# A graph network's ODE solver with its two weight products per step folded into one: six-layer local pass, mid stages without a product

## The reference, cut to what matters

```
def gcn(x, W, b):                    # edges src -> dst, deg = edges in + 1, dinv = rsqrt(deg)
    h = x @ W
    agg = segment_sum(h[src] * (dinv[src] * dinv[dst]), dst)
    return agg + dinv * dinv * h + b
x = l2norm(gcn(nodes, W1, b1))                                   # 128 -> 256
def f(z):
    return gcn(l2norm(gcn(z, Wf1, bf1)), Wf2, bf2) + z           # 256 -> 256 -> 256
k1 = f(x); k2 = f(x + 0.5*k1); k3 = f(x + 0.5*k2); k4 = f(x + k3)
x = x + (k1 + 2*k2 + 2*k3 + k4) / 6
y = gcn(x, W2, b2)                                               # 256 -> 128
x = layernorm(nodes + y)
x = layernorm(x + attention(x, edge_attr))
```

## Time and profile before

| | us |
|---|---|
| median of three runs | 7468.84 (7468.58 to 7469.83) |
| profiled execution, span | 7463.9 |
| TensorE busy | 6262.2 (84%) |
| VectorE busy | 6114.0 (82%) |
| GpSimd busy | 4840.9 (65%) |
| ScalarE busy | 3838.3 (51%) |

### The profile page before, as it was taken

The page is one execution under the profiler, slowest core; times in us unless marked ns, Lnnn a source line. Parts: engine busy times, 40 slices in busy tenths (PEclk is TensorE's granted clock), DMA queues, the critical chain, the costliest instruction groups (busy, mean ns, idle before and its releaser), DMA issues. The chain is left out here.

```text
span 7463.9 us, 156875 instructions
## 1 busy us (share of the span) xinstructions
PE 6262.2 (84%) x37260; PEld 5197.7 (70%) x37260; DVE 6114.0 (82%) x15796; ACT 3838.3 (51%) x10696; POOL 4840.9 (65%) x5469
## 2 busy tenths in 40 slices
PE   7699889899999657989989998999888765877776
PEld 3588888888889436867766676667666554865664
DVE  8588778787888777889879977997799887878887
ACT  6466666666666576733661166116622233654443
POOL 0488888888873576855776577657744565546665
PEclk8799999999999899999999999999999998988998
DMA  0365555554444466879779977997799765543432
GB/s 2 102 165 161 161 160 158 162 161 152 146 145 152 146 190 199 247 257 297 229 223 332 329 226 224 331 327 228 230 385 387 259 186 151 152 138 119 125 123 86
DMA packets 981268, 1483.74 MB, mean 199 GB/s; under 512 B 156967, under 2 KB 450705, under 8 KB 980647
## 3 DMA queue, kind: packets, MB, share of 16 engines
q1 hardware_dynamic: 685479, 922.39, 37.2%
q0 software_dynamic: 141504, 309.42, 16.2%
q10 hardware_dynamic: 153664, 244.12, 9.0%
HBM read 902.58 MB, written 573.11 MB: 198 GB/s over the span
## 5 line engine op out<-in xcount | busy, mean ns | idle before, releaser
L1336 PE MATMUL bank<-c_rows,sums_all 128*128 128x256 f32 (+1 forms) x3920 | 1320.9, 420 | 550.5 <-DVE c_rows L1487 304.3
L751 PE MATMUL bank<-wf_w,c_xt 128*128 128x256 f32 x6272 | 1615.0, 381 | 2.0 <-DVE y L1545 2.0
L1381 ACT ACTIVATE c_xt<-bank 128x512 f32<-128x512 f32 (+1 forms) x980 | 556.8, 568 | 1586.6 <-issue 831.0
L1307 POOL DMA_INDIRECT c_rows<-t_tab,src_pair x784 | 870.2, 1110 | 705.6 <-PE bank L1336 546.2
L1336 PEld LDWEIGHTS bank<-c_rows,sums_all 128*128 128x128 f32 x3920 | 633.9, 194 | 984.7 <-DVE c_rows L1487 478.7
L751 PEld LDWEIGHTS bank<-wf_w,c_xt 128*128 128x128 f32 x6272 | 1133.7, 191 | 127.0 <-ACT c_xt L1381 3.5
L1487 DVE SCALAR_TENSOR_TENSOR c_rows<-bank,carry,c_rows 32x256 f32<-32x256 f32 (+1 forms) x1950 | 913.7, 469 | 274.3 <-PE bank L1336 117.6
L1307 POOL DMA_INDIRECT c_rows<-z_tab,src_pair x784 | 770.7, 983 | 293.3 <-issue 189.5
L1085 DVE TENSOR_TENSOR lx_lo<-bank,lx_hi 128x512 fp32r<-128x512 f32 (+1 forms) x1000 | 658.6, 659 | 260.6 <-ACT lx_hi L1030 217.4
L1030 ACT ACTIVATE lx_hi<-bank 128x512 fp32r<-128x512 f32 (+1 forms) x1000 | 569.4, 572 | 580.4 <-PE bank L999 418.6
L741 PE MATMUL bank<-wf_hi,lx_hi 128*128 128x256 f32 x3200 | 725.0, 309 | 62.7 <-issue 49.4
(11 more groups left out here) (333 smaller groups left out, 14629.2 us busy)
## 6 DMA issues: line engine op xcount, KB each, us to landing
c_z<-z_tab SPq DMA_DIRECT2D x882, 256.0 KB
z_tab<-lz SPq DMA_DIRECT2D x400, 256.0 KB
t_tab<-lt SPq DMA_DIRECT2D x400, 256.0 KB
z_tab<-y ACTq DMA_DIRECT2D x392, 256.0 KB
c_own<-z_tab SPq DMA_DIRECT2D x392, 256.0 KB
t_tab<-y ACTq DMA_DIRECT2D x392, 256.0 KB
c_own<-t_tab SPq DMA_DIRECT2D x392, 256.0 KB
fl_x<-x_tab SPq DMA_DIRECT2D x396, 128.0 KB
```

Of the source, the lines that this page charges most:

```text
L751: last = nc.tensor.matmul(out, x(k), w[:, k, :], start=(k == 0), stop=(k == ks - 1 and not bias))
L1307: pool.indirect_dma_start(out=rows[:, s, i, 0:win], out_offset=None, in_=source, in_offset=bass.IndirectOffsetOnAxis(ap=m["src_i"][:, t:t ...
L1336: nc.tensor.matmul(psum[s % 2][:, i * win:(i + 1) * win], sums[:, j * 2 + i, :], rows[:, s, i, 0:win], start=True, stop=True).then_inc(S[" ...
L1381: nc.scalar.activation(xt[:, s % 2].rearrange("p k n -> p (k n)")[:, 0:n], psum[2 + s % 2][:, 0:n], ACT.Copy).then_inc(S["copied"], 1)
```

## The change

The solver's linear part is folded. With W21 = Wf2 Wf1 / 2 and W22 = Wf2 W2 / 6 made on chip, a step keeps one product in place of two. The table z_tab is replaced by p_tab (z times Wf1), and the mid stages only add up, scale and store. The final product with W2 is shared between a part of z that the first stage makes (`q_tab`) and the tail of the fourth step.

- `split_weights` becomes `fuse_weights`: loads, transposes, products and copies, and bias rows `vec_rows`, `vec_parts`.
- The local pass has six layers (C = 6, 24 slots in a block), full-word products throughout, no low parts. Layer 1 makes two products (Wf1 and W2). Each layer stores p and t (256 KB each).
- Powers on GpSimd are made for two steps at once (128x4), the clamp moves to VectorE.
- The operations of the edge tables are issued in each non-zero layer one or two to a step (`table_turns`).
- The first coupled stage also turns and multiplies its result (z_turn, z_multiply, take_p, take_q), and rows are 129 wide, for a sum of weights.
- A new block `coefficients` follows it: twelve small DMAs.
- The mid stages have no transpose, copy, product or take. A 3-row bias matmul precedes each addition (for the second tile, after the wait for the carry).
- The first three end stages multiply by W21, with the bias matmul for both tiles, ScalarE scales the product and VectorE adds the rest; they also store `u_tab` (256 KB per pair, from SP).
- The fourth (`tail`) loads three u tables and `q_tab`, multiplies by W22, and stores 128 wide. The last stage gathers 128 wide and has no product.
- The rings on y have eight slots.

```diff
+def table_turns(at, layer):
+    if layer == 0:
+        return 0
+    return 1 if at % 3 == 0 else 2
...
+def fuse_weights(nc, a, S, m):
...
+                for kc in range(2):
+                    for km in range(2):
+                        last = nc.tensor.transpose(psum[0][:, kc * H2 + km * P:kc * H2 + (km + 1) * P],
+                                                   wf2[:, km, kc * P:(kc + 1) * P], ident[:])
+                last.then_inc(S["w_fused"], 1)
+                pe.wait_ge(S["w_copied"], 1)
+                for w, bank, width in ((m["wf1_w"], psum[1], H2), (m["w2_w"], psum[2], D)):
+                    for km in range(2):
+                        for kc in range(2):
+                            last = nc.tensor.matmul(bank[:, km * width:(km + 1) * width],
+                                                    wf2_turned[:, kc, km * P:(km + 1) * P], w[:, kc, :],
+                                                    start=(kc == 0), stop=(kc == 1))
...
-    G, C = 4, 10
+    G, C = 4, 6
...
-                        nc.gpsimd.tensor_tensor(inv[:, h, :], ss[:, h, :], neg_half[:], ALU.pow
-                                                ).then_inc(S["inverted"], 1)
-                    if layer[q] != 0:
+                    elif side:
+                        pool.wait_ge(S["clamped"], ph.at("clamped", b, q))
+                        nc.gpsimd.tensor_tensor(inv[:, k, :, :], ss[:, k, :, :], neg_half[:], ALU.pow
+                                                ).then_inc(S["inverted"], 2)
+                    for _ in range(table_turns(at[0], layer[q])):
                         next(tables, None)
-                staggered(pool, blocks, Q, early, [(0, gather_x), (12, invert)], unrolled=True)
+                staggered(pool, blocks, Q, early, [(0, gather_x), (10, invert)], unrolled=True)
...
-                staggered(sp, blocks, Q, early,
-                          [(0, load_rows), (3, load_again), (5, keep), (16, store), (17, store_own), (18, store_sums)],
+                staggered(sp, blocks, Q, early,
+                          [(0, load_rows), (3, load_again), (5, keep), (10, store_own), (11, store_sums), (16, store_taken),
+                           (20, store_done)],
...
+                    w, ks, width, vec = [("w1", 1, H2, None), ("wf1", 2, H2, None), ("w21", 2, H2, STEP),
+                                         ("w21", 2, H2, STEP), ("w21", 2, H2, STEP), ("w22", 2, D, ENDS)][c]
                     for i in range(2):
+                        last = full_product(nc, psum[4 + n][:, i * width:(i + 1) * width],
+                                            lambda k: xt[:, n, k, i * P:(i + 1) * P], m[w + "_w"], ks,
+                                            (m["ones_r"][:], m["vec_parts"][:, vec[0]:vec[1]]) if vec else None)
+                    if c == 1:
+                        for i in range(2):
+                            last = full_product(nc, psum[n][:, i * D:(i + 1) * D],
+                                                lambda k: xt[:, n, k, i * P:(i + 1) * P], m["w2_w"], 2)
-                staggered(pe, blocks, Q, early, [(0, turn), (2, multiply)])
+                staggered(pe, blocks, Q, early, [(0, turn), (1, multiply)])
...
-                staggered(act, blocks, Q, early, [(0, high), (6, scale), (1, begin_rest), (4, square)])
+                staggered(act, blocks, Q, early, [(0, copy), (6, scale), (2, take_share), (3, square)])
...
-                staggered(dve, blocks, Q, early, [(6, normalise), (1, low), (3, add_rest), (3, take), (0, build)])
+                staggered(dve, blocks, Q, early, [(8, normalise), (0, combine), (4, clamp), (2, add_rest), (2, take),
+                                                  (0, build)])
...
+                    if i == 1:
+                        pe.wait_ge(S["carried"], ph.at("carried", j, 2))
+                    if mid:
+                        nc.tensor.matmul(out, degs[:, s % 4, i * P:(i + 1) * P], vec_rows[0:3, vec[0]:vec[1]],
+                                         start=True, stop=False)
+                    if i == 0:
+                        pe.wait_ge(S["carried"], ph.at("carried", j, 1))
+                    nc.tensor.matmul(out, sums[:, j * 2 + i, :], rows[:, s % 4, i, 0:wide], start=not mid, stop=True
+                                     ).then_inc(S["summed"], 1)
...
+            def z_multiply(j, s):
+                pe.wait_ge(S["z_copied"], ph.at("z_copied", j))
+                if past(j, 1):
+                    pe.wait_ge(S["p_taken"], ph.at("p_taken", j - 1))
+                for w, bank, width in ((m["wf1_w"], psum[7], H2), (m["w2_w"], psum[(3, 6)[s % 2]], D)):
+                    for i in range(2):
+                        last = full_product(nc, bank[:, i * width:(i + 1) * width],
+                                            lambda k: m["c_zt"][:, s % 2, k, i * P:(i + 1) * P], w, 2)
+                last.then_inc(S["p_product"], 1)
-            skewed(pe, pairs, [(0, add_up(0)), (2, turn), (3, multiply(0)), (0, add_up(1)), (3, multiply(1))],
+            steps = [(0, add_up(0)), (0, add_up(1))]
+            if multiplied:
+                steps = [(0, add_up(0)), (2, turn), (3, multiply(0)), (0, add_up(1)), (3, multiply(1))]
+            if first:
+                steps += [(8, z_turn), (9, z_multiply)]
+            skewed(pe, pairs, steps, ring=8, unrolled=True)
...
+            if first:
+                steps = [(2, copy), (0, scale_own), (8, z_copy), (6, scale), (9, take_q), (4, square), (11, store_both)]
+            elif mid:
+                steps = [(4, scale), (4, store), (2, square)]
+            elif final:
+                steps = [(6, normalise), (6, store)]
+            else:
+                steps = [(2, copy), (4, draw), (6, store)]
...
+            if first:
+                steps = [(0, carry_on(0)), (1, add_own), (0, carry_on(1)), (5, clamp), (4, take), (10, take_p)]
+            elif mid:
+                steps = [(0, carry_on(0)), (1, add_own), (0, carry_on(1)), (3, clamp)]
+            elif tail:
+                steps = [(0, carry_on(0)), (1, add_rest), (1, add_own), (0, carry_on(1)), (5, take)]
+            elif final:
+                steps = [(0, carry_on(0)), (2, add_rest), (1, add_own), (0, carry_on(1)), (3, clamp), (2, take), (6, shift)]
+            else:
+                steps = [(0, carry_on(0))] + ([(4, add_rest)] if n_rest else []) + \
+                    [(1, add_own), (0, carry_on(1)), (5, take)]
```

More of the change, by code:

```diff
@@ L736, in product @@
-def product(nc, out, hi, lo, w_hi, w_lo, ks, bias=None):
-    n, last = 0, None
-    for x, w in ((hi, w_hi), (hi, w_lo), (lo, w_hi)):
-        for k in range(ks):
-            last = nc.tensor.matmul(out, x(k), w[:, k, :], start=(n == 0), stop=(n == 3 * ks - 1 and not bias))
-            n += 1
-    if bias:
-        last = nc.tensor.matmul(out, bias[0][:], bias[1][:], start=False, stop=True)
-    return last
+                for k in range(2):
+                    last = v.tensor_scalar(bf2_wide[:, k, :], ident[:], 0.0, bf2_col[:, k:k + 1], ALU.mult, ALU.add)
@@ L1228, in coupled_stage @@
     v, psum, ident = nc.vector, m["psum"], m["ident"]
-    own, rows, sums, y, u, rest = (m[n] for n in ("c_own", "c_rows", "sums_all", "y", "c_u", "c_rest"))
-    degs, deg_hi, deg_lo = (m[n] for n in ("c_degs", "c_deg_hi", "c_deg_lo"))
-    scaled_bias = m["c_bias"]
-    turned_degs = mid and r == 0
-    begun = end and r in (0, 3)
-    by_pe = [(), (0,), (0,), (0, 1)][r] if end else ()
-    by_dve = [i for i in range(2) if i not in by_pe] if end else []
-    xt, ss, inv = (m[n] for n in ("c_xt", "c_ss", "c_inv"))
@@ L1252, in past @@
+    ph8 = counts.phase(pairs, {"t_stored*": 0 if first else 16}, ring=8)
+    done = "done" if rooted else "taken"
     def past(j, n):
@@ L1319, in _ @@
                 pool.wait_ge(S["c_constants"], 1)
-            for j in range(pairs + (8 if rooted else 0)):
+            behind = 6 if mid else 8
+            for j in range(pairs + (behind if rooted else 0)):
                 if j < pairs:
                     gather(j, j % 4)
-                if rooted and j >= 8:
-                    invert(j - 8, j % 4)
+                if rooted and j >= behind and j % 2:
+                    invert(j - behind)
         @block.tensor
@@ new lines, in add_own @@
+                for i in range(2):
+                    out = y[:, s, i, :] if mid else u[:, s % 4, i, 0:win]
+                    last = v.scalar_tensor_tensor(
+                        out, psum[s % 2][:, i * wide:i * wide + win], m["lead"][:, bass.ds(j * 2 + i, 1)],
+                        u[:, s % 4, i, 0:D] if first else own[:, s % 4, i, 0:win], ALU.mult, ALU.add)
+                if tail:
+                    last.then_inc(S["combined"], 1)
+                    dve.wait_ge(S["combined"], ph.at("combined", j))
+                    last = v.scalar_tensor_tensor(u[:, s % 4, :, :], rest[:, s % 2, :, :], SUMS[2], u[:, s % 4, :, :],
+                                                  ALU.mult, ALU.add)
```

1012 lines of the change are left out of this document (580 added, 432 removed).

## The result

The changed kernel takes 7823.5 us (median of 4 runs, 7820.9 to 7834.6) against 7469.3 us beside it: a ratio of 1.048, interval 1.046 to 1.049, 354 us slower. The profiled execution has a span of 7832.9 us, 369 more than the 7463.9 of before, and the stages account for all of it. It was the longest of the four (7834.6 from outside), 11 us above the median, which is most of what 369 has over 354.

What follows compares the result with a forecast made beforehand. It took TensorE, with GpSimd nearly full, to bound the local pass, and the pace of a pair the coupled stages. Terms summed to +223 on the 7463.9 us span, 7687, with 5 around it 7692 us; range 7340 to 7850.

Steps and rivals of the forecast that it cites:

- a loop in the first stage closed by take_p: First coupled stage: next z product waits for take_p of the pair before, 6.5 us per pair, stage 677 us, +303.
- rival (a): Mid stages run at full clock, additions 0.70 us in place of 1.22: 7397 us in all, chance 0.25.
- rival (b): The clock rises in about half of the mid stages: 7542 us in all, chance 0.10.
- Rival (c): TensorE falls to half clock in the first stage as well, 230 us longer: 7920 us in all, chance 0.05.
- (d): First stage's loop does not bind, as squares run before take_q: -211, 7480 us in all, chance 0.04.
- Local pass, -523: Local pass and weights: six layers for ten, GpSimd setting the pace, pass 1702 us against 2234, with weights -523.
- First stage and coefficients, +323: First coupled stage slowed by its loop to 677 us, +303, and the new coefficients block, +20.
- Mid stages, +347: Four mid stages at half clock, bound by the carry chain: 4.1 us per pair, 427 us each, +347.
- Ends, +147: First three end stages: first +71 from product and bias sequence, second and third +76 from DMA at 372 GB/s.
- Tail, -19: Fourth end stage: less DMA, VectorE 4.4 us per pair, 4.5 with waits, 466 us for 485, -19.
- Last, -52: Last stage: no product and 128-wide rows, 378 us for 430, -52.
- Attention and finish, 0: Attention and finish: only names of semaphores change, 0.

Runs made afterwards that it cites:

- Experiments 1: Changed kernel plus four idle matmuls per pair in the mid stages, two behind each addition: 7606.0 us, ratio to before 1.017.
- experiment 4: Changed kernel, first coupled stage: VectorE does take_p before clamp and take, 7685.9 us; ScalarE also does squares before take_q, 7689.3 us.
- Experiment 2: Changed kernel plus 24 idle matmuls ahead of the first addition of each mid stage: 7889.4 us.
- Experiment 6: Changed kernel, tail only: VectorE carries into the second tile before its own addition and not after: 7768.6 us.
- experiment 7: Changed kernel with all helpful edits and idle matmuls in mid, tail and last stages: 7261.7 us with two per mid-stage pair, 7277.3 with three.

## Why the prediction was right, and where its terms were off

The forecast was 7692 with a range of 7340 to 7850, and 7823.5 is slower and inside. The mechanism that decided the sign was the right one: mid stages at half clock, additions of 1.22, and a loop in the first stage closed by take_p. Experiments 1 and 4 show both by taking them away. The number owes something to luck: local pass, mid stages, tail and attention came out 238 us above the forecast, first stage, ends and last 92 below it, and only the difference shows in the sum. The range had to be as wide as 510 us, since it held rival (a) as well.

The forecast gave two reasons for the half clock: the mid stages begin after an idle stretch, and they never have a run of products. Experiment 2 gave them a run of matmuls at the start, and they fell back all the same. So what keeps them slow is the thin work itself, and the start is not a reason of its own.

Rival (a), the full clock by itself, is refuted by the windows at 0.50, and experiment 2 shows that a better start would not bring it about; rival (b) falls too, as no mid stage rose in part. Rival (c) did not come about (0.97 in the first stage), and (d) is refuted by experiment 4.

- **Local pass, -523, measured -417.** GpSimd did set the pace, and its sum was good: up to 1950, when its table operations are all but through (step 566 in the forecast), its operations and the gaps behind them make 1585 us, where 1597 was forecast. What failed is that its waits were put at nothing: in the same stretch it stands about 100 us waiting for VectorE's clamp, at the start and again and again later. With TensorE busy 81% of 600 to 1400 (at a clock of 0.91), the two are late by turns. The upper bound named this (1850). The block of weights took 12 us and not 19.
- **First stage and coefficients, +323, measured +300.** The loop held, 6.45 for 6.5. From the last take_q of the stage (2732.4) to the first gather of the next stage 18 us pass, with the coefficients in them, for which 20 was taken.
- **Mid stages, +347, measured +414.** The period was 4.35 and not 4.1. The second bias costs 0.51 and not 0.45, and the chain alone takes 3.89 and not 3.66. The row of 3.66 had the same work in it, VectorE's own additions (L1501) included, but shorter pauses of TensorE, 0.64 and 0.59 us for 0.70 and 0.79. One of those own additions, and the addition on TensorE that follows the shorter pause:

```profile
3207.99 0.85 DVE L1501 SCALAR_TENSOR_TENSOR c_u<-bank,lead,c_own 128x256 f32<-128x256 f32 x2
3209.92 1.22 PE L1336 MATMUL bank<-c_rows,sums_all 128*128 128x256 f32 x2 [0.59 <-issue]
```

Why the pauses grew is open.

- **Ends, +147, measured +87.** The forecast took 372 GB/s for the limit of DMA. Over 300 us of the second end stage the trace moves more:

```profile
4100.00:4400.00 300.00, 300.00 (x1338) 212.94 (x1339) 226.07 (x447) 98.33 (x222) 146.41 (x150) 1.00 1.04 391
```

TensorE is the bound, without a gap, at (418 - 25) / 98 = 4.01 per pair: the 4.05 of the sequence in the earlier trace rows, without the allowance for slack. The first end stage bears this out: it moves less (306 GB/s, a DMA share of 0.92) and takes the same 418 us.

- **Tail, -19, measured +33.** The sum of VectorE's work (4.4) was right, its order was not looked at. Between two carries it does four pieces of other work, 2.9 us, as its timeline in the tail shows, and TensorE waits 1.87 us for the second carry. Experiment 6 gives 60 us back, more than the 52 that were missed, with the clock at 0.88 in place of 0.81. (The forecast's 1.54 MB a pair are 4.14 us at 372 GB/s and not 4.24; nothing hangs on it.)

```profile
5961.05 0.47 DVE L1705 SCALAR_TENSOR_TENSOR c_rows<-bank,carry,c_rows 32x256 f32<-32x256 f32 x1 [0.46 <-PE bank L1513]
...
5964.79 0.49 DVE L1705 SCALAR_TENSOR_TENSOR c_rows<-bank,carry,c_rows 32x256 f32<-32x256 f32 x1
```

- **Last, -52, measured -61**, at a clock of 0.51, which the forecast did not name; idle matmuls there brought it from 369 to 354.
- **Attention and finish, 0, measured +13.** Not pursued. The same code differs by 13 us between the two kernels of experiment 7 as well.
- One sentence misreads a row: the 0.86 us of the earlier trace rows is the full-word product of one tile, not of two. The sums use 1.72 for two and are not touched by it.

## What to carry to other kernels

Taking work from TensorE can cost time, when what is left is thin and on a serial chain: price such a stage at the slow clock, and try a few idle matmuls behind each link before giving the change up. Before adding up an engine's work for a new loop, write down for each engine what stands in its list ahead of the step that releases the next turn; here two single moves in such lists were worth 140 and 60 us. Where two engines are each nearly full, the sum for either is a lower bound and not the pace: give the waits between them a term. And count what passes between an engine's operations as well as the operations, since GpSimd at 79% busy was 95% in use.

## What was not expected of the hardware

The clock fell from 1.00 to 0.50 within six microseconds after the burst, in work that had no pause over 0.61 us (experiment 2). DMA held 391 GB/s over 300 us. The same code of the local pass took between 1799 and 1859 us in eight traces, a spread of 3% in a kernel whose whole time repeats within 0.2% in one set of runs.
